# A decoder layer with routed experts on one core: masks ahead of the placing on VectorE, the last cross exponentials in the next step, router and output projection moved within the odd step

## What is computed

```python
x = layernorm(x + self_attention(x))                  # 16 heads of 64, causal, softmax
x = layernorm(x + cross_attention(x, ctx, mask))      # 16 heads of 16, key mask, biases
def moe_group(x2, router_w, wg, wu, wd, top_k=2):     # 16384 tokens, 32 experts
    scores = softmax(x2 @ router_w)
    w, idx = top_k(scores, 2)
    ys = (silu(xs @ wg[e]) * (xs @ wu[e])) @ wd[e]    # xs: the tokens sorted by expert e
    return sum over the token's two experts of w * ys
x = layernorm(x + (2 * moe_group_0(x) + 2 * moe_group_1(x)) / 4)
```

## Time and profile before

| | |
|---|---|
| median of three runs | 5197.35 us |
| profiled execution: its time, and its span from first to last instruction | 5205.27 us, 5203.4 us |
| TensorE busy | 4658.9 us, 90% |
| VectorE busy | 3827.1 us, 74% |
| ScalarE busy | 3274.2 us, 63% |
| GpSimd busy | 2779.5 us, 53% |
| mean granted TensorE clock | 0.974 of full |

### The profile page before, as it was taken

How to read it: one execution, slowest core, us unless ns; L and a number is a source line. 1 busy time by engine, 2 the same in 40 slices (tenths; PEclk the granted TensorE clock), 3 DMA queues, 4 the chain that set the end, 5 groups by cost and what they waited for, 6 DMA issues and landing times. The chain is left out here.

```text
span 5203.4 us, 129007 instructions
## 1 busy us (share of the span) xinstructions
PE 4658.9 (90%) x37824; PEld 3986.0 (77%) x37824; DVE 3827.1 (74%) x18185; ACT 3274.2 (63%) x12613; POOL 2779.5 (53%) x3874
## 2 busy tenths in 40 slices
PE   8988888888888888888888888888888789999998
PEld 7777777777777777777777777777777567877876
DVE  4777777777777777777777777777777736665888
ACT  6766666666666666666666666666666534444444
POOL 3455555555555555555555555555555545556777
PEclk9999999999999999999999999999999889999999
DMA  4111111111111111111111111111111459997998
GB/s 154 50 54 54 55 55 54 59 55 54 54 54 54 55 55 54 54 54 56 55 54 54 54 54 55 59 57 54 54 54 50 141 178 343 333 305 251 310 306 288
DMA packets 477418, 552.04 MB, mean 106 GB/s; under 512 B 55632, under 2 KB 408144, under 8 KB 476240
## 3 DMA queue, kind: packets, MB, share of 16 engines
q1 hardware_dynamic: 350800, 296.21, 17.9%
q0 software_dynamic: 52224, 146.87, 7.6%
q10 hardware_dynamic: 73728, 100.70, 6.4%
HBM read 266.21 MB, written 277.35 MB: 104 GB/s over the span
## 5 line engine op out<-in xcount | busy, mean ns | idle before, releaser
L875 ACT ACTIVATE prob<-prob,negmax 128x128 f32<-128x128 f32 x2048 | 796.8, 393 | 701.2 <-DVE negmax L991 701.2
L875 ACT ACTIVATE xprob<-xprob,xnegmax 128x128 f32<-128x128 f32 x2048 | 800.5, 402 | 10.1 <-DVE xnegmax L991 10.1
L1324 POOL DMA_INDIRECT y_d<-y,to x576 | 565.0, 981 | 366.0 <-DVE y L1466 287.7
L569 POOL CAST yTh<-yT 128x512 fp32r<-128x512 f32 x256 | 171.9, 671 | 1022.2 <-ACT yT L911 1022.2
L624 POOL DMA_INDIRECT xs_d<-xrow,place x512 | 541.2, 1057 | 133.6 <-issue 133.6
L991 DVE CUSTOM_DVE_ANT_0 prob<-bank,causal 128x128 f32<-128x128 f32 x2048 | 451.2, 283 | 204.2 <-PE bank L750 204.2
L1377 PE MATMUL bank<-moe,xgT 128*128 x2304 | 597.6, 382 | 1.0 <-issue 0.6
L588 POOL TENSOR_TENSOR rs<-spread_v,minus_half 128x1 f32<-128x1 f32 x256 | 145.4, 568 | 681.1 <-DVE spread_v L1064 681.0
L1027 DVE TENSOR_TENSOR prob<-prob,inv 128x512 f32<-128x512 f32 x512 | 461.7, 902 | 17.6
L1036 DVE RECIPROCAL xinv<-xtotal 128x4 f32<-128x4 f32 x512 | 87.7, 171 | 520.7 <-ACT xprob L875 520.7
L777 PE MATMUL bank<-ident,prob 128*128 128x128 f32 x2048 | 311.2, 275 | 172.6 <-DVE negmax L991 172.5
(11 more groups left out here) (173 smaller groups left out, 14570.0 us busy)
## 6 DMA issues: line engine op xcount, KB each, us to landing
xg<-xs_d SPq DMA_DIRECT2D x576, 129.0 KB
xs_d<-blank SPq DMA_DIRECT2D x248, 272.0 KB, 2.8
rows<-y_d ACTq DMA_DIRECT2D x256, 256.0 KB
xT_s<-xT SPq DMA_DIRECT2D x128, 128.0 KB
cT<-cT SPq DMA_DIRECT2D x128, 128.0 KB, 2.1
x_s<-x SPq DMA_DIRECT2D x128, 128.0 KB, 2.1
x_d<-x SPq DMA_DIRECT2D x128, 128.0 KB, 1.9
sums<-x_d ACTq DMA_DIRECT2D x128, 128.0 KB
```

The source lines that it names most:

```text
L569: nc.gpsimd.tensor_copy(yT_p[0][:, c, :], yT[:, :, :]).then_inc(y_high, 1)
L875: last = nc.scalar.activation(dst[:, h, :], dst[:, h, :], ACT.Exp, bias=src_bias[:, h:h + 1], scale=-1.0, accum_out=acc[:, h:h + 1])
L1324: nc.gpsimd.indirect_dma_start(y_d[:, :], bass.IndirectOffsetOnAxis(ap=to[:, m % NTO:m % NTO + 1].bitcast(U32), axis=0), y_s[q][:, :], Non ...
```

## The change

The instructions stay the same ones but for a copy of four numbers per token (`xrow[..., OWNER]`), which goes from VectorE to ScalarE. What changes is the order and where a thing is done:

- VectorE: `place_tokens` and `rank_moves` no longer stand ahead of the masks; both are at the end of the odd double-step, `rank_moves` in the same one as TensorE's rank job, which has moved from the even into the odd double-step. `cross_normalise(n, 1)` comes in the next double-step, behind the masks. In the even one the copy of x1T goes ahead of `weigh`, of the second `normalise` and of x2; in the odd one x2T is copied ahead of `normalise(n, 0)`, and x1 is made before the placing.
- ScalarE: the exponentials of cross side 1 are done at the start of the next double-step; in the odd one `move_qk(n, "qk3")` goes behind the first cross copy.
- TensorE: in the odd double-step o1 stands ahead of the first `cross_turn`, and route ahead of qk3. Several waits that others imply are taken out.
- GpSimd: `open_blocks`, `scatter` and `root(0)` change places, as below; `hot` has two buffers, and three small tables share memory.

```diff
-EVEN = ("qk0", "o2", "qk1", "x1t", "v1", "xq", "xv", "rank", "xy")
-ODD = ("qk2", "x2t", "qk3", "o1", "route", "xk", "v0", "xy")
+EVEN = ("qk0", "o2", "qk1", "x1t", "v1", "xq", "xv", "xy")
+ODD = ("qk2", "x2t", "o1", "route", "qk3", "xk", "rank", "v0", "xy")
-AFTER = dict(... rank=10)
+AFTER = dict(... rank=11)
@@ GpSimd, double_step @@
-                        b = due(n, 11, NB)
+                        b = due(n, 14, NB)
+                        if b is not None:
+                            scatter(b, (2, 3))
+                        b = due(n, 12, NB)
                         if b is not None:
                             open_blocks(b)
-                        b = due(n, 12, NB)
-                        if b is not None:
-                            scatter(b, (0, 1))
                         if split_pair(n) is not None:
                             x_low(split_pair(n))
                         b = due(n, 8, NB)
                         if b is not None:
                             root(1, b)
+                        b = due(n, 3, NB)
+                        if b is not None:
+                            root(0, b)
                         b = due(n, 13, NB)
                         if b is not None:
-                            scatter(b, (2, 3))
+                            scatter(b, (0, 1))
...
@@ TensorE, score (cross_score likewise) @@
                         if g == 0:
-                            for name in QK:
-                                pe.wait_ge(moved[name], b + 2 - b % 2)
-                        wait(pe, maxed, 2 * n)
-                        wait(pe, probT_in, 2 * (n - 1))
+                            pe.wait_ge(moved["qk3"], b + 2 - b % 2)
+                        if not live(n - 2):
+                            wait(pe, maxed, 2 * n)
+                            wait(pe, probT_in, 2 * (n - 1))
@@ TensorE, double_step, odd @@
                             turn(n, 1)
+                            job(n, "o1")
+                            cross_turn(n, 0)
+                            job(n, "route")
                             job(n, "qk3")
-                            cross_turn(n, 0)
-                            job(n, "o1")
                             cross_turn(n, 1)
-                            job(n, "route")
                             job(n, "xk")
+                            job(n, "rank")
                             job(n, "v0")
@@ ScalarE @@
+                    def owners(n):
+                        b = due(n, 10, NB)
+                        if b is None:
+                            return
+                        act.wait_ge(route_step, b * 6 + 6)
+                        wait(act, placed[b % 2], b // 2 * PLACED)
+                        nc.scalar.copy(xrow[b % 2][:, :, OWNER], choice[b % 2][:, :, :].rearrange("p g k -> p (g k)")).then_inc(owner_in, 1)
...
                     def double_step(n):
                         move_y(n)
+                        cross_exponentials(n - 1, 1)
                         exponentials(n, 0)
...
@@ VectorE @@
                     def even_step(n):
-                        place_tokens(n)
                         masked(n)
                         cross_masked(n)
+                        cross_normalise(n - 1, 1)
...
                         if b2 is not None:
                             variance(steps2, 1)
-                        weigh(n)
+                        move_transposed(n, "x1t")
                         normalise(n, 1)
...                                                   # x2, waiting for root(1)
-                        move_transposed(n, "x1t")
+                        weigh(n)
                         cross_normalise(n, 0)
...
-                        cross_normalise(n, 1)
                     def odd_step(n):
-                        rank_moves(n)
                         masked(n)
                         cross_masked(n)
+                        cross_normalise(n - 1, 1)
+                        move_transposed(n, "x2t")
                         normalise(n, 0)
-                        move_transposed(n, "x2t")
...
                         normalise(n, 1)
-                        cross_normalise(n, 0)
                         b1 = job_of(n, "o1")
                         if b1 is not None:
                             steps1 = residual(n, "o1", 0, norm1_step, sum1, x_s, x_in, (b1 + 1) * 16)
+                            variance(steps1, 0)
                         top_two(n)
...
+                        place_tokens(n - 1)
+                        rank_moves(n)
+                        cross_normalise(n, 0)
```

More of the change, by code:

```diff
@@ L655, in double_step @@
                             token_rows(b)
-                        b = due(n, 3, NB)
-                        if b is not None:
-                            root(0, b)
                     steps_of(double_step)
@@ L846, in double_step @@
                             job(n, "xv")
-                            job(n, "rank")
                         else:
@@ L1071, in rank_moves @@
                         dve.wait_ge(made["rank"], b + 1)
-                        rank, count = (jb(n - 1, "rank")[:, c:c + NE].rearrange("p (g e) -> p g e", g=NGRP) for c in (0, NE))
+                        rank, count = (jb(n, "rank")[:, c:c + NE].rearrange("p (g e) -> p g e", g=NGRP) for c in (0, NE))
                         wait(dve, first_ready, b)
```

56 lines of the change are left out of this document (29 added, 27 removed).

## The result

The changed kernel takes 4846.27 us (median of four runs, 4841.9 to 4848.55), the kernel before on the same chip 5193.44 (four runs, 5183.77 to 5199.1): a ratio of 0.9332 [0.9315, 0.9349], faster by 347 us. The forecast was 4725 in a range of 4660 to 4855.

What follows compares the result with a forecast made beforehand. TensorE's pair period, 32.07 us, was taken to bound the kernel: 31.40 - 1.37 - 2.10 + 0.2 gives 28.1, saving 472 us over 119 periods; 5205.3 becomes 4733, and 8 less for the median is 4725 us, range 4660 to 4855.

Steps and rivals of the forecast that it cites:

- its neighbourhood: Whole kernel: the forecast together with a stall of 0 to 0.7 us per pair, 4673 to 4785 us, chance 0.65.
- signs of being wrong: First stage: TensorE's waits on a new cause exceed 1 us per pair, or the x1T copies' period is above 29.
- The two waits go (1.37 and 2.10): TensorE's waits per pair, 1.37 us for the row minima before the first transposes and 2.10 for x1T before xq, disappear.
- The base of 27.93: First stage, us per pair of double-steps without TensorE's two waits: 31.40 - 1.37 - 2.10 = 27.93.
- the rival of a clean TensorE: First stage: no wait is left on TensorE, 27.7 us per pair, 4673 us in all; chance 0.17.
- The copy of four numbers at 0: ScalarE, end of the even step: the copy taken over from VectorE runs near +10.5 and costs 0.
- o1, route, qk3 and rank at 0: TensorE: the moved jobs have their inputs and banks in time, the work is the same, the cost 0.
- `root(1)` at +9 and x2's wait of 1.2: Even step: GpSimd starts `root(1)` near +9 and ends it near +9.7; VectorE, ready at +8.5, waits 1.2 for it.
- The wait of `cross_score` then lies between 0 and 0.7: TensorE, odd step's cross scores: waiting for xq takes 0 to 0.7 us per pair, of which 0.2 was taken.
- three losses of 0.6: VectorE behind `root(1)`: three operations losing 0.6 each beside GpSimd put xq at +14.9 instead of +13.0.
- The clock's 0.67 goes: First stage: the 0.67 us per pair lost to a lower clock after some 2.10 us waits disappears.
- The ring as a rival: GpSimd-VectorE loop sets the pair: 29 to 29.4 us if each odd-step multiply loses 0.7, 4855 us; chance 0.13.

Runs made afterwards that it cites:

- p1: Kernel before, with only the exponentials of cross side 1 and their normalisation moved into the next double-step: 4885.22 us, ratio 0.9413.
- p2: Kernel before, with only the copy of x1T moved ahead of `weigh`, the second normalisation and x2: 4913.15 us, ratio 0.9471.
- a8: Changed kernel with the copy of x1T put back behind x2: 5084.53 us, ratio 0.9799 to the kernel before.
- a7: Changed kernel with the exponentials and normalisation of cross side 1 back in their own step: 5037.19 us, ratio 0.9708 to the kernel before.
- a1: Changed kernel with `root(1)` on GpSimd ahead of `open_blocks`: 4646.29 us, ratio 0.8951 to the kernel before.
- a5: Changed kernel with the odd step's order of o1, route and qk3 as before: 5060.88 us, ratio 0.9755 to the kernel before.
- a3: Changed kernel with `x_low` on VectorE in place of GpSimd: 4694.71 us, ratio 0.9044 to the kernel before.
- a2: Changed kernel with `weigh` ahead of x2 on VectorE: 4664.24 us, ratio 0.8986 to the kernel before.
- p3: Kernel before, with the edits of p1 and p2 together and nothing else of the change: 4686.67 us, ratio 0.9034.
- a4: Changed kernel with SyncE's clearing of the block rows ahead of its loads: 4846.76 us, ratio 0.9335 to the kernel before.

## Why the prediction was right in sign and short by 121 us

The forecast of 4725 with its neighbourhood (4673 to 4785) was missed. The 4846 lie in the full range, 9 us from its upper end, and that end came from a rival with a chance of 0.13. Two of the prediction's own signs of being wrong came true: waits on a new cause exceed 1 us a pair (1.1 in the mean), and the period is above 29 (29.12). The clock of the stage is 0.99 and not 1.00, and TensorE is busy for 96% of it and not 99%.

**The two waits go (1.37 and 2.10): right.** Both are gone. The first self exponential is at +2.18 (forecast +2.2), the copy of x1T ends at +7.94 (+7.7). p1, p2 and a8 show that each move does its part, and a7 that the exponentials' move is needed for the chain to xqT as well. What the prediction gave to the placing's move, though, the exponentials' move does alone (p1).

**The base of 27.93: 0.2 too high.** Short pairs take 27.70, which was the term of the rival of a clean TensorE; a1 takes 27.57.

**The copy of four numbers at 0: right.** It runs 0.22 on ScalarE at +10.56 (forecast +10.5), and taken back it costs 0.07 at most.

**o1, route, qk3 and rank at 0: wrong as a reading of what they do.** All waits were met, as it said. But the larger part of their worth isn't in TensorE's own waits: they make the placing early, and o1, route and qk3 taken back cost 215 us (a5). I had priced a move by whether its inputs are ready, and not by who waits for its output. Rank was not tried alone.

**`root(1)` at +9 and x2's wait of 1.2: right in the short pair** (+9.45, 1.29), not in the long one (+10.48, 2.23).

**"The wait of `cross_score` then lies between 0 and 0.7", and 0.2 taken: this step failed.** It is 0 in 58 of 119 periods and 2.1 to 2.5 in the others, 1.1 in the mean. The upper end was the sum of x2 at +9.7, 3.2 from there to xqT and three losses of 0.6 (13.0 and 1.8 are 14.8, not 14.9). The chain behind x2 was inside that: it takes 3.8 in the short pair and 5.0 in the long one, with 0.4 lost on x2, 0.8 on `weigh`'s first operation, and in the long pair 0.3 more in `weigh` and 0.9 on the cross multiply. (The 1.40 for `weigh` already held a loss of some 0.6; its work alone is 0.8.) What was outside is the start of x2, +11.08 in the long pair, 1.4 later than forecast. I took all even pairs as alike and let the lateness begin at the even score. It begins in the odd step before, with `x_low`: 1.1 on VectorE's multiply passes the placing and the odd step's scatters, and in the even step it makes the scatters lose 0.7 too. The a3 run shows this origin, a1 and a2 show the link.

**The clock's 0.67 goes: three fifths right.** Of the 119 periods 17 still lose 1.4 to 1.7 and two 3.4 (0.27 in the mean), since the waits of 2.1 are still there.

The sum with the measured terms: 27.70 + 0.51 x 2.22 + 0.27 = 29.10, against 29.12 counted. The 29.12 less the forecast 28.1, times 119, is 121 us, and 4846 - 4725 = 121.

**The ring as a rival** had a chance of 0.13, 29 to 29.4 a pair and 4855. A ring is what came: from the odd cross scores through placing, scatters, `split_y`, `root(1)`, x2 and xqT to the next odd cross scores. It is 29.91 long (2025.22 to 2055.13) where `x_low` is in it, and in the short pair it fits with 0.05 to spare. But the rival let each of the odd step's multiplies lose 0.7 in all pairs alike; one multiply loses 1.1 in every second odd step, and the rest is lost in the even step. That the mean of 27.70, 29.92 and the clock's loss falls on its 29.2 is in part luck. I had counted 25.4 to 27.3 for the ring without such losses. One thing that I left out is the delay of 0.76 between the placing's end and the first scatter. The ring deserved more than 0.13, since the count left it 0.8 of room and the rows already showed single losses of 0.7.

**Not predicted at all:** a better version lay beside it. p3 takes two of the moves and is 160 us faster than the change; the change with `root(1)` ahead of `open_blocks` is 200 us faster. The eight instructions ahead of the root are in the prediction's own sum, 2.1 of 9.7, and nothing waits for them in that step. The second stage starts 8 us later than it need, too: the wait for the tables is 34.8 to 35.0 in all runs made from the changed kernel, and 26.9 in the kernel before and in p1, p2 and p3.

## What to carry to other kernels

When a wait on the bounding engine is removed, write out the ring that its reader closes through the other engines, with each shared-port loss and each DMA start in it, for every kind of step; with two kinds of step the later one decides, not the mean. Price a moved job by who waits for its output, and look first at small work that nobody waits for and that stands ahead of what everybody waits for. When a change has many parts, try the two that answer to the two largest waits alone: here they gave more than the whole.

## What the runs showed of the hardware

- From 200 to 3600 us, each of the 128x512 multiplies of VectorE that took over 1.0 us instead of 0.69 (118 in the changed kernel, 156 in the kernel before) ended 0.54 to 0.55 behind the end of the GpSimd instruction during which it had started.
- A scatter issued by GpSimd that starts inside a two-input multiply of VectorE takes longer. In the changed kernel, from 200 to 3600 us, the 112 that do take 1.23 to 1.48 us, and the other 356 take 0.97 to 1.09, but for one of 1.21. The added time goes with what the multiply has still to run: 0.45 where that is 0.6, 0.25 where it is 0.4. The Trainium skill's "SBUF — State Buffer", section "SBUF: two separate sides", says that such transfers can't write their descriptors while VectorE holds the port pair in a two-port mode, and infers that an operation with two inputs leaves them alone. Here it is a multiply with two inputs that makes them longer, and the measurement decides.
- The first scatter started 0.76 us behind the end of the placing that released it (2007.57 to 2008.33, 2036.39 to 2037.15), with GpSimd idle; one that follows work on GpSimd starts 0.15 to 0.3 behind it. a4 shows that the clearing transfer has no part in it; what the 0.76 is made of stays open.
- The clock over 2000:3000 was 1.00 in the kernels whose waits were 1.4 to 1.8 us (p1, p2), and 0.97 to 0.99 in those with waits of 2.0 to 3.0 (the change, a5, a7, a8), though only some of these waits were followed by a lower clock: 19 of 61 in the 119 periods of the change.
- A lateness grew from 1.1 to 2.2 on its way, since it decides who is first at the shared port.
